# Attention mixing turned round: probabilities move, 32-column value tiles stand, one 128x512 reciprocal for four heads

## The reference, cut to what matters

```python
q = _rope(split_heads(_conv(_mcl(x, Wq, bq), q_conv_w, q_conv_b, 3)))
k = _rope(split_heads(_conv(_mcl(x, Wk, bk), k_conv_w, k_conv_b, 3)))
v = split_heads(_conv(_mcl(x, Wv, bv), v_conv_w, v_conv_b, 3))
qk = jnp.einsum('bceqd,bcekd->bceqk', q, k) / math.sqrt(h)
a = jax.nn.softmax(qk, axis=-1)
o = jnp.einsum('bceqk,bcekd->bceqd', a, v)
```

## Time and profile before

| | us |
|---|---|
| median of 2 runs | 1271.07 (1269.8 to 1272.35) |
| profiled execution, its own time | 1263.9 |
| its span | 1262.0 |
| busy: PE / DVE / POOL / ACT | 1106.7 / 965.2 / 874.2 / 655.4 |
| mean granted clock of PE | 0.960 |
| `attend`, about | 406 to 997 |

### The profile page before, as it was taken

How to read it: one execution, slowest core, us unless ns; L and a number is a source line. 1 busy time by engine, 2 the same in 40 slices (tenths; PEclk the granted TensorE clock), 3 DMA queues, 4 the chain that set the end, 5 groups by cost and what they waited for, 6 DMA issues and landing times. The chain is left out here.

```text
span 1262.0 us, 30504 instructions
## 1 busy us (share of the span) xinstructions
PE 1106.7 (88%) x12696; PEld 752.7 (60%) x12696; DVE 965.2 (76%) x1466; ACT 655.4 (52%) x1078; POOL 874.2 (69%) x812
## 2 busy tenths in 40 slices
PE   0299999999893888999999999999999589999997
PEld 0177777777672145666667666666667444455553
DVE  3789899999763998988898888988873385544344
ACT  1555555555332176666666666666666223346345
POOL 0467777777584499988998888988889005947900
PEclk9899999999897599999999999999989899999999
DMA  9825234331654455445352707162000499975661
GB/s 303 254 79 153 87 111 121 98 111 47 139 132 124 66 89 142 69 79 94 81 97 58 122 28 143 34 115 57 27 19 18 130 365 316 269 256 161 194 208 54
DMA packets 137778, 159.30 MB, mean 126 GB/s; under 512 B 17853, under 2 KB 85709, under 8 KB 137641
## 3 DMA queue, kind: packets, MB, share of 16 engines
q1 hardware_dynamic: 113448, 119.37, 38.8%
q10 hardware_dynamic: 15648, 28.81, 6.5%
q0 software_dynamic: 8544, 9.18, 2.7%
HBM read 106.48 MB, written 52.89 MB: 126 GB/s over the span
## 5 line engine op out<-in xcount | busy, mean ns | idle before, releaser
L1106 POOL TENSOR_TENSOR a_pl<-a_prob 128x512 bf16<-128x512 f32 x416 | 452.0, 1113 | 54.8 <-ACT a_prob L1063 50.7
L1063 ACT ACTIVATE a_prob<-a_col 128x512 f32<-128x512 f32 x512 | 303.0, 597 | 187.2 <-PE a_col L953 176.3
L1007 DVE TENSOR_REDUCE a_negmax<-a_row 128x1 f32<-128x512 f32 x512 | 336.6, 694 | 48.1 <-PE a_row L931 47.6
L710 POOL TENSOR_TENSOR f_yl<-f_y,f_yh 128x768 bf16<-128x768 f32 x80 | 132.8, 1679 | 93.0 <-ACT f_yh L657 93.0
L970 PE MATMUL a_mix<-a_vp,a_prob 128*128 128x65 bf16 x2048 | 195.5, 195 | 1.1 <-DVE a_o L1032 0.9
L970 PEld LDWEIGHTS a_mix<-a_vp,a_prob 128*128 128x128 bf16 x2048 | 163.7, 99 | 53.5 <-issue 5.2
L971 PE MATMUL a_mix<-a_vp,a_pl 128*128 128x65 bf16 x2048 | 193.9, 195 | 0.0
L971 PEld LDWEIGHTS a_mix<-a_vp,a_pl 128*128 128x128 bf16 x2048 | 146.4, 99 | 60.4 <-issue 4.4
L657 ACT ACTIVATE f_yh<-f_y 128x768 bf16<-128x768 f32 x80 | 67.4, 844 | 138.9 <-DVE f_y L548 120.2
L450 PE MATMUL f_acc<-f_wh,f_xh 128*32 128x384 bf16 x1280 | 109.9, 332 | 28.0 <-DVE f_wl L538 25.9
L931 PE MATMUL a_row<-k,q 96*128 96x512 bf16 x256 | 108.3, 429 | 29.0 <-PEq L202 15.0
(11 more groups left out here) (153 smaller groups left out, 2356.8 us busy)
## 6 DMA issues: line engine op xcount, KB each, us to landing
X<-b_x ACTq DMA_DIRECT2D x16, 526.0 KB, 8.2
q<-in_x SPq DMA_DIRECT2D x8, 1024.0 KB, 7.5
a_v<-V SPq DMA_DIRECT2D x16, 512.0 KB, 4.4
Z<-a_z ACTq DMA_DIRECT2D x32, 256.0 KB, 2.7
b_z<-Z SPq DMA_DIRECT2D x16, 512.0 KB, 11.2
b_x<-in_x SPq DMA_DIRECT2D x32, 256.0 KB, 9.9
b_res<-X SPq DMA_DIRECT2D x38, 208.0 KB
out<-b_y ACTq DMA_DIRECT2D x38, 208.0 KB
```

What stands on the lines that cost most here:

```text
L710: nc.gpsimd.tensor_tensor(yl[half][n % 2][:], y[half][:], yh[half][n % 2][:], ALU.subtract).then_inc(yl_done, 1)
L1007: nc.vector.reduce_max(negmax[u][:, QT * h + qt:QT * h + qt + 1], row[row_buffer(h, qt)][:], AX.X, negate=True).then_inc(max_done, 1)
L1063: nc.scalar.activation(prob[head % PROBS][:, kt, :], col[kt % 2][:], ACT.Exp).then_inc(exp_done, 1)
L1106: nc.gpsimd.tensor_tensor(pl[head % PROBS][:, kt, :], prob[head % PROBS][:, kt, :], ph[head % PROBS][:, kt, :], ALU.subtract).then_inc(lo_ ...
```

## The change

Four heads are now handled as a set. In `mix_set` the value tile of a head, 128x32, is stationary, and the probabilities move, 512 columns at once; the four heads of a set go to the partitions 0, 32, 64 and 96 of one PSUM tile `a_mix`, so features lie on partitions and positions along the row. The denominators come from eight more matmuls of a set with a stationary tile of ones (128x32) into a second PSUM tile `a_weight`, where each denominator stands 32 times. Each set is of one tile of 128 keys: 20 matmuls of 512 columns, and a unit has 8 sets (2 groups of four heads by 4 tiles of keys), issued in every fourth slot.

`invert` becomes one reciprocal of 128x512 for four heads, and `divide` one multiplication of 128x512 into `a_oT`, two of each for a unit. `a_o`, the eight adding and turning parts of `tail` and their two copies on ACT go; the projection's eight parts stay. `split_max` loses its first instruction, since the high part of the maxima is taken as a view. Of the steps, 6 of 32 low parts stay on DVE (every fifth), and 26 on POOL. The lookahead of three rows now holds across units too (it was two at a unit's first three rows). The slots, modulo 32: sets at 22, 26, 30, 2, 6, 10, 14, 18; `invert` and `divide` at 3 and 19; `split_max` at 0; low parts of DVE at 3, 8, 15, 20, 25, 30; `tail` at 21 to 24 and 26 to 29.

```diff
+            def mix_set(n, g):
+                kt, quad = g % QT, SETS // QT * n + g // QT
+                p = (SETS * n + g) % RING
+                pe.wait_ge(lo_pool, pool_lows(n, g))
+                pe.wait_ge(lo_dve, dve_lows(n, g))
+                if kt == 0 and quad:
+                    pe.wait_ge(inverted, quad)
+                for part in (ph, pl):
+                    for r in range(QUAD):
+                        nc.tensor.matmul(weight[r * DH:(r + 1) * DH, :], ones[:], part[p][:, r, :],
+                                         start=kt == 0 and part is ph, stop=kt == QT - 1 and part is pl)
+                if g == 0:
+                    pe.wait_ge(v_lo, n + 1)
+                if kt == 0 and quad:
+                    pe.wait_ge(divided, quad)
+                for j, (vv, part) in enumerate(((vh, ph), (vl, ph), (vh, pl))):
+                    for r in range(QUAD):
+                        h = g // QT * QUAD + r
+                        last = nc.tensor.matmul(mix[r * DH:(r + 1) * DH, :], vv[n % 2][:, kt, h * DH:(h + 1) * DH], part[p][:, r, :],
+                                                start=kt == j == 0, stop=kt == QT - 1 and j == 2)
+                last.then_inc(mixed, 1)
...
-                    if j < FH:
-                        last = nc.tensor.matmul(out[:, at], o[u % 2][:, part, n, j * P:(j + 1) * P], ident[:], start=n == 0, stop=n == 1)
...
+                    if j == 0:
+                        pe.wait_ge(divided, SETS // QT * (n + 1))
...
+            def invert(n, m):
+                quad = SETS // QT * n + m
+                ve.wait_ge(mixed, QT * (quad + 1))
+                nc.vector.reciprocal(inverse[quad % 2][:], weight[:]).then_inc(inverted, 1)
+
+            def divide(n, m):
+                quad = SETS // QT * n + m
+                if m == 0 and n >= 2:
+                    ve.wait_ge(out_full, FH * (n - 1))
+                ve.wait_ge(inverted, quad + 1)
+                nc.vector.tensor_tensor(oT[n % 2][:, m, :], mix[:], inverse[quad % 2][:], ALU.mult).then_inc(divided, 1)
...
-        EXP = TURN + 7
-        MIX = EXP + 3 * QT
-        NORM = MIX + QT
-        TAIL = 3 * STEPS + 5
...
+        MIX = EXP + 3 * QUAD
+        KEEP = MIX + QUAD * (QT - 1) + 1
+        TAIL = KEEP + QUAD * QT + 2
```

## The result

The changed kernel takes 1420.17 us (median of 2 runs, 1417.1 to 1423.25) against 1271.07: a ratio of 1.118, with an interval of 1.113 to 1.123. It is slower, as predicted, but by 149 us where 43 were forecast, and it lies above the range (1237 to 1368).

A forecast was written before the change was run, and what follows sets the result against it. No engine bound it by share: PE paced the tail stretch, DVE the other. 15 x (36.2 + 0.8 - 33.7) = +49.5, less 6, gave +43: 1263.9 became 1307, plus 7 made 1314 us; range 1237 to 1368.

The forecast's parts named there:

- Where the stop is: In `attend`, PE goes three rows ahead, then waits for `inverted` and `divided` at slots 6, 21 and 22.
- The rival of the hidden pause: PE has enough rows ahead to hide at most 1.8 us at each place: 1260 us, no change; chance 0.07.
- The shape on PE: In `mix_set`, four matmuls run side by side in 0.216 us; with switching a set takes 1.28 us.
- The rival of half speed: Strided probabilities move at half speed in PE's sets: +30 us, 1344 us in all; chance 0.08.
- R: Length of each 128x512 reciprocal on DVE, two a unit, taken at 2.8 us from 5.3 ns an element.
- the long divide: Rival: the reciprocal on DVE takes 4.3 us, making 39.2 + 0.8 us a unit and 1360 us; chance 0.25.
- The clock, 0.8 us a unit: Half clock on PE after its two pauses a unit in `attend`: half of 1.6 us taken as added.
- upper bound of 1.6 us: Most that PE's low clock adds to a unit, from one unit of 35.3 us, not 33.6, in the earlier trace.
- The base, 30.6 us: A unit of `attend` without its two reciprocals; with them it is 30.6 + 2R = 36.2 us, against 33.7 before.
- the split's part: DVE's remaining work for the split in each unit, taken at 0.9 us in the stretch to `divide`.
- the two handovers of 0.25 us: Handovers added to the DVE and PE stretches of each unit: about 0.25 us each, 0.5 together.
- The ends, -6 us: After the last mixing about -3 us, and 3 us of the previous unit's tail in the draining stretch: together -6.

The follow-up runs named there:

- e1: Changed kernel with the 128x512 reciprocal replaced by a plain copy on the same engine, the division left out: 1271.27 us, ratio 0.999.
- e3: Changed kernel with 16 matmuls that nobody reads on PE ahead of each wait for the inverse and the division: 1353.59 us, ratio 1.062.
- e11: Changed kernel with the reciprocal replaced by a copy and DVE's six low parts a unit left out: 1247.04 us, ratio 0.979.
- e14: Changed kernel with a copy as reciprocal, no DVE low parts, and sets one slot later between column and row score: 1246.61 us, ratio 0.978.
- e2: Changed kernel with the reciprocal on columns 0 to 255 only, the other 256 a plain copy: 1356.49 us, ratio 1.064.
- e9: Changed kernel with a copy as reciprocal and DVE's six low parts moved to steps 9 to 19, every second: 1282.66 us, ratio 1.007.

## Why the direction was right and the size was not

**Where the stop is: right.** The prediction had PE run out of rows at the tail of slot 21 and at the set of slot 6. The two waits of after stand exactly there, once each in a unit (62.0 us in 16 waits for `a_oT`, 52.0 for `a_inverse`). The rival of the hidden pause is out: from e1 to e3 a unit grows by 4.8 us for 5.3 us more of instruction, so the length is paid nearly in full.

**The shape on PE: right.** Four matmuls of 32 stationary columns start 0.22 to 0.23 us after the last four, also those that move `ph` with its elements 4 bytes apart (748.34, 748.56 and 748.79 in after: `a_mix` from `a_prob` and `a_vh`, `a_prob` and `a_vl`, `a_pl`). The rival of half speed is out. The switch between a set and a score costs 0.1 us as taken (748.79 to 749.12 is 0.33, not 0.22). Two multiplications of 0.61 us each are right as well.

**R, 2.8 us: too small by 0.55.** That is 1.1 us a unit, 16 us in all. The slope of 4.7 to 4.8 ns rested on differences of 15 ns; it is 6.3. The measured R lies between the forecast and the long divide (4.3 us), within the forecast's own span of 1.8 to 3.6. The Trainium skill (VectorE: DVE Perf Modes, "First, the fixed hardware budget") read as 8 cycles an element gave 4.3 us; the measurement is 3.35, so that reading doesn't hold.

**The clock, 0.8 us a unit: wrong by 3.5, some 52 us, the largest term of the miss.** It measured 4.3 us. The failed step is its upper bound of 1.6 us. That came from one short dip in the earlier trace rows, after a pause of less than a microsecond, and I took it for the worst that a pause could do. Here PE stops for 3.5 to 4.2 us, and works for 6.1 and 9.1 us at half clock behind it. The prediction named the case among what would make it wrong ("if the clock falls for more than a short stretch in each unit"), but gave it neither a chance nor a price. The trace of before had the evidence, ahead of the last unit: PE waits 0.90 and 1.44 us close together, the clock falls within the second wait, and it stays low from 934.8 to 941.7, nearly 7 us.

```profile
933.41 0.19 PE L970 MATMUL a_mix<-a_vp,a_prob 128*128 128x65 bf16 x1 [0.90 <-DVE a_o L1032]
935.26 0.60 PE L943 MATMUL a_out<-a_ident,a_maxparts 128*16 128x128 bf16 x4 [1.44 <-DVE a_maxparts L1015]
...
935.00:941.00 6.00, 5.74 (x47) 4.37 (x48) 3.58 (x7) 2.74 (x5) 3.40 (x5) 0.50 0.01 3
```

The clock alone would not have carried the result out of the range: 1314 + 52 = 1366 us lies just inside the upper end of 1368. It took the other terms as well, and all of them erred to the same side.

**The base, 30.6 us: too small by 1.8.** With the clock kept and R measured the sum gives 37.3, and e3 has 39.1: 27 us in all. In e1 the gap is 2.5. Two steps failed. The first is the work of DVE. Its low parts were taken at 1.0 us each; their mean is 134.8 / 96 = 1.40, where before had 106.1 / 96 = 1.10 for the same instruction; that some wait for POOL's is shown, why more of them do than before is not. The other way, the split's part was taken at 0.9 us and takes 0.17 here, so the two errors partly cancel. And the low parts can't be the whole gap: the sum without its three would be 28.8 us, and e11 without all six has 32.9. The second step is the two handovers of 0.25 us, taken for all that PE waits beyond the sum: in e14, where little else holds PE up, its waits for other engines are 2.4 us a unit, and a further 1.4 lie in the sets' cycle. A sum of two engines' busy work fitted before to 1%; it did not carry over to a structure with one set for four heads. That each wait holds a larger piece there is a likely reason, but no run shows it.

**The ends, -6 us: wrong.** In the profiled execution they are +15. The part behind the last value instruction grew by 2.0; there the clock is halved too, and the projection's 16 matmuls take

```profile
1138.11 3.78 PE L995 MATMUL a_out<-a_oT,a_wo 128*128 128x128 f32 x16 [4.19 <-DVE a_oT L1033]
```

where the earlier trace rows has 2.05. In e1, without the stops, the same part is 40.6 us, 9 less than before, so the saving was real. In e3, with the reciprocal and the clock kept, it is 49.1: the length took 8.5 us of it, the clock another 2.6. The rest is 6.7 us ahead of the first unit (the first row score comes at 414.0 in place of 406.1) and 5.9 behind the stage, in code that the change doesn't touch; why it takes longer isn't shown.

Added up: 27 + 16 + 52 = 95 us in the units, 21 at the ends, and 10 less since this profiled execution lies 3 us above its median and that of before 7 below: 106, the distance from 1314 to 1420.

## What to carry to other kernels

A long instruction on one engine is paid twice if it makes TensorE stop: once as the wait, and again as work at half clock behind it, which here was nearly as dear (4.3 us a unit against 4.8). So when a change merges many short operations into a long one, ask what the engine ahead of it can do meanwhile, and bound the price of its clock by half of the time that TensorE may work at half clock afterwards, taken from the longest low stretch in the trace and not from the shortest. Measure a structure first with the costly instruction replaced by a cheap one; here one such run shows that there was nothing to gain even with an inverse as short as a copy.

## What the runs showed of the hardware

- VectorE's reciprocal out of PSUM takes 3.35 us for 128x512 and 1.74 for 128x256, against 0.68 for a copy of 128x512.
- In stops of TensorE of 3.5 to 3.7 us the clock falls to 1.2 GHz 0.7 and 1.0 us before TensorE starts again, and it comes back after 6.1 us of work in one place and 9.1 in another. Stops of 2.2 to 2.4 us (e2) bring the low clock too (0.87). Matmuls that nobody reads, put into the stop, keep it at 2.4 GHz: 1.00 with 16 of them, 0.94 with 8.
- A subtraction of VectorE with two operands in SBUF takes 0.68 us when POOL is idle and up to 2.7 in after beside POOL's; in e9, while POOL worked without a gap, one in nearly every unit lasted 4.3 us and one 9.0.
- Loading a table on ScalarE takes 1.28 us; 64 loads cost 143 us here, more than the 82 us of ACT's time that they fill. The clock fell with them (0.84 against 0.97 without), and what it cost is within the 143.
